# The first attention group opens on its short row tiles, with the bias fold moved to the last body

## The chip, the cores and the metric

The kernel runs on one core of a Trainium2 chip. The time is the device time of one launch, in microseconds (us), and the median of several runs is compared. The profile is of one further execution, and its times count from the start of that execution's span.

## The reference, cut to what matters

The input is x with 4 batches of 1024 rows of 128 features. A layer norm with modulation gives h. Then comes causal attention with 16 heads of size 8, whose scores have two parts:

```
scores = Q K^T / sqrt(8) + lambda * (tanh(Q) J) tanh(K)^T
scores = where(causal, -inf, scores)
probs  = softmax(scores);  out = probs V;  x = x + ga * (out Wo + bo)
```

A second norm gives each row to one of 8 experts, and row by row

```
ln = norm(xs) * gamma_e + beta_e
y  = xs + relu(ln W1_e^T + b1_e) W2_e^T + b2_e
```

is mixed back into x. Since beta_e only enters through W1_e, the product of W1_e with beta_e can be added to b1_e once and for all. That sum is the bias fold that the change moves.

## The kernel before, in words

**Groups and slots.** Each batch is one pass ("body"): batch 0 is the body "first", 1 and 2 are "middle", 3 is "last". A body has 4 groups of 4 heads. A group of attention is 12 units, and a unit is a pair of a query half `qc` (512 queries) and a block `kb` of 128 keys. Each unit has 4 slots, one a head, so that a group has 48 slots. Units 0 to 3 are the first query half, and so are slots 0 to 15. In a slot TensorE makes the transposed scores (L1258), adds the causal mask on diagonal blocks (L1262), and ScalarE takes the exponential (L1014). Two units later TensorE multiplies by the values (L1232).

**Maxima.** Before a group can start, the row maxima of its scores must be known, since they ride as three extra rows of the query stack into L1258. They are made by score products of another orientation (L1192), by chunks: a chunk is one or more heads of a row tile `t`, which has (t+1)*128 columns. Chunks with t from 4 to 7 are long (16 of them, one head each). VectorE reduces one with L1672. Chunks with t from 0 to 3 are short (6 of them, with 2 or 4 heads), reduced by L1679. After all 22 chunks of a group comes the step "T": TensorE turns the maxima (L1180), VectorE splits them into three bf16 terms (L1657 to L1663), and SyncE sends them into the stack (`send_maxima`, L426). TensorE waits for them with `m_in` in slot 0.

**The order around the change.** TensorE and VectorE each run one written-out order. `FIRST` is what comes before the first attention group: ten projections ("P": X0 to V1 of batch 0), the 22 chunks of group 0, two chunks of group 1, T of group 0, and four more chunks of group 1. Between them TensorE turns the expert weights (`turn_weights`, L1209), six after the projections and then one behind each chunk. ScalarE evacuates them, and SyncE stores them in two DMAs (L463). In a body, `schedule` places the next group's chunks behind slots, by a table of costs, and in group 0 also the ten projections of the next batch. ScalarE evacuates X, Q, K and J of those, and it makes the eight normalised row tiles of the next batch (L903) behind slots 1 and 3 of units 0 to 3.

**The fold.** GpSimd makes the folded bias in the prelude (`fold_beta`, L662 to L673) from W1, which is loaded for the turning, and from beta, which ScalarE's queue broadcasts into the tile `OT`. ScalarE waits for the fold (`b1_ok`) ahead of its first attention group, since it then writes `OT`, and GpSimd makes it ahead of its work on batches 0 and 1.

## Time and profile before

| | us |
|---|---|
| median of 3 runs (773.18 to 775.75) | 775.23 |
| the profiled execution | 773.26 |
| its span | 771.5 |
| TensorE busy | 676.7 (88%) |
| VectorE busy | 545.0 (71%) |
| ScalarE busy | 500.7 (65%) |
| GpSimd busy | 258.0 (33%) |

Read this as shares of the whole span. The stages differ: a prelude up to some 84 us, 16 attention groups up to some 640 us, and the expert part after that.

### The profile page before, as it was taken

What the parts mean: (1) busy time and instruction counts of PE and PEld (TensorE: products, weight loads), DVE (VectorE), ACT (ScalarE), POOL (GpSimd) and SP (SyncE); (2) the same over time, 40 slices, a digit from 0 to 9 for tenths busy, and PEclk for the clock granted to TensorE, in tenths of its full rate; (3) what the DMA queues carried; (4) which work ended last, traced back from release to release, by engine and by line L of the source; (5) the groups of instructions that cost most, each with busy time, mean ns of one, the idle gap of its engine ahead of it and who ended that gap; (6) DMA issues with size and microseconds to landing.
All of it is one profiled execution on the core that took longest, in us unless ns stands there. A gap on an engine that the chain in (4) does not pass through costs nothing.

```text
span 771.5 us, 15278 instructions
## 1 busy us (share of the span) xinstructions
PE 676.7 (88%) x5199; PEld 341.3 (44%) x5199; DVE 545.0 (71%) x1249; ACT 500.7 (65%) x1182; POOL 258.0 (33%) x342
## 2 busy tenths in 40 slices
PE   3657899999999998999999989999998989887693
PEld 2352344333333433433344434343443227886593
DVE  6959666887866786778667868788777603897352
ACT  1431577766767866766877586866767788655472
POOL 2009109200201943513138234210352202466443
PEclk9867699999999999999999999999999999999797
DMA  8996732456533251925606165636313445424610
GB/s 224 316 206 240 131 68 64 131 98 113 118 67 60 71 178 32 177 56 148 124 1 193 58 112 97 157 94 129 97 43 112 161 142 169 126 78 146 177 40 11
DMA packets 55572, 91.88 MB, mean 119 GB/s; under 512 B 10257, under 2 KB 26157, under 8 KB 55240
## 3 DMA queue, kind: packets, MB, share of 16 engines
q1 hardware_dynamic: 49308, 79.72, 41.6%
q0 software_dynamic: 3520, 8.42, 3.1%
q10 hardware_dynamic: 2668, 2.78, 1.3%
q8 instruction: 42, 0.69, 0.4%
q14 instruction: 34, 0.28, 0.1%
HBM read 51.04 MB, written 37.90 MB: 115 GB/s over the span
## 4 chain that ended last, share of the span: by engine, by line
PE 54%; DVE 20%; ACT 12%; issue 7%; DMA 4%; another core or an unknown queue 1%; ACTq 1%; DVEq 0%; POOL 0%; SPq 0%; POOLq 0%
PE PS L1232 15%; PE PS L1192 12%; PE PS L1258 11%; ACT arenaA L1014 7%; DVE PS L1672 6%; PE PS L1309 4%; PE PS L1320 3%; DVE block_max L1679 3%; ACT arenaB L932 2%; PE PS L1262 2%; DVE arenaA L1355 2%; DVE arenaB L1355 2%; PE PS L1197 1%; PE PS L1140 1%
## 5 line engine op out<-in xcount | busy, mean ns | idle before, releaser
L1014 ACT ACTIVATE arenaA<-PS 128x512 f32<-128x512 f32 (+3 forms) x768 | 332.4, 498 | 157.3 <-PE PS L1262 119.9
L1672 DVE CUSTOM_DVE_ANT_0 PS<-PS,mask 128x1024 f32<-128x1024 f32 (+3 forms) x256 | 261.4, 1035 | 90.4 <-PE PS L1192 85.4
L1258 PE MATMUL PS<-arenaA 99*128 99x512 bf16 (+3 forms) x768 | 221.5, 332 | 14.9 <-ACT arenaA L1014 11.6
L1192 PE MATMUL PS<-arenaA 96*128 96x512 bf16 (+3 forms) x768 | 198.8, 335 | 26.0 <-DVE maxima L1672 8.2
L1258 PEld LDWEIGHTS PS<-arenaA 99*128 99x128 bf16 x768 | 71.6, 97 | 202.5 <-ACT arenaA L1014 141.6
L1232 PE MATMUL PS<-arenaA,Vs 128*9 128x512 f32 (+3 forms) x1536 | 158.3, 488 | 0.0
L1679 DVE TENSOR_REDUCE block_max<-PS 128x8 f32<-128x1024 f32 (+1 forms) x96 | 100.4, 1045 | 28.8 <-PE PS L1197 26.1
L1192 PEld LDWEIGHTS PS<-arenaA 96*128 96x128 bf16 x768 | 66.7, 100 | 90.9 <-DVE maxima L1672 31.3
L1262 PE MATMUL PS<-after,identb 128*128 128x128 bf16 x512 | 104.5, 221 | 0.0
L1063 ACT ACTIVATE arenaA<-PS,b1p 128x128 f32<-128x128 f32 x184 | 52.6, 374 | 35.3 <-PE PS L1309 21.2
L831 POOL DMA_INDIRECT out_dram<-arenaA x46 | 46.1, 1002 | 82.7 <-DVE arenaA L1355 73.8
L1309 PE MATMUL PS<-arenaA 128*128 128x128 f32 x368 | 51.3, 284 | 11.8 <-DVE arenaA L1792 8.7
L1309 PEld LDWEIGHTS PS<-arenaA 128*128 128x128 f32 x368 | 45.4, 194 | 16.0 <-DVE arenaA L1792 12.3
L1320 PE MATMUL PS<-arenaA 128*128 x368 | 50.3, 282 | 1.9 <-issue 1.9
L1262 PEld LDWEIGHTS PS<-after,identb 128*128 128x128 bf16 x512 | 50.6, 99 | 2.3
L1197 PE MATMUL PS<-identb,after 128*128 128x128 bf16 x256 | 50.2, 224 | 0.0
L772 POOL DMA_INDIRECT by_expert<-arenaB,slot x24 | 23.5, 979 | 72.2 <-PE PS L1232 72.2
L1320 PEld LDWEIGHTS PS<-arenaA 128*128 128x128 f32 x368 | 46.1, 197 | 2.5 <-issue 2.4
L1232 PEld LDWEIGHTS PS<-arenaA,Vs 128*9 128x9 f32 x1536 | 24.6, 88 | 51.0 <-ACT arenaA L1014 26.2
L643 POOL TENSOR_TENSOR arenaB<-arenaB 128x1024 f32<-128x1024 f32 x12 | 25.6, 2133 | 55.6 <-ACT arenaB L873 55.6
L1355 DVE TENSOR_TENSOR arenaA<-PS,b_b 128x128 f32<-128x128 f32 x46 | 13.4, 290 | 33.6 <-PE PS L1320 21.7
L1672 DVE DVE_READ_ACCUMULATOR2_ANT maxima<- 128x1 f32 x256 | 35.7, 139 | 0.2
(219 smaller groups left out, 691.1 us busy)
## 6 DMA issues: line engine op xcount, KB each, us to landing
arenaA<-k_parts SPq DMA_DIRECT2D x96, 128.0 KB, 8.0
arenaA<-by_expert SPq DMA_DIRECT2D x46, 192.5 KB
o_raw<-OT SPq DMA_DIRECT2D x32, 256.0 KB, 2.1
k_parts<-arenaB SPq DMA_DIRECT2D x24, 256.0 KB, 3.8
arenaA<-q_parts SPq DMA_DIRECT2D x16, 384.0 KB, 5.2
q_parts<-arenaB SPq DMA_DIRECT2D x18, 256.0 KB, 3.8
arenaA<-in_L_ffn_W_dram SPq DMA_DIRECT2D x2, 2048.0 KB, 12.9
arenaA<-q_parts SPq DMA_DIRECT2D x16, 256.0 KB, 5.7
```

Of the source, the lines that this page charges most:

```text
L831: g.indirect_dma_start(out_rows, bass.IndirectOffsetOnAxis(ap=XSI[n % NX][:, 3 * D:3 * D + 1], axis=0), YS[:, n % U, :], None, bounds_chec ...
L1014: a.activation(PT[:, u % EB, h, off:HALF], PS[:, 4 + n % SB_, off:HALF], ACT.Exp).then_inc(exp_ok, 1)
L1063: last = a.activation(HR[:, n % 3, k * P:(k + 1) * P], PS[:, 3 + n % 2, k * P:(k + 1) * P], ACT.Relu, bias=b1p[:, bass.ds(expert[n] * FC + ...
L1192: last = mm(PS[:, place + c0 // HALF, at:at + c1 - c0], SQ(g, h)[0:KROWS, t * P:(t + 1) * P], SK(g, h)[0:KROWS, c0:c1], start=(at == 0), s ...
L1197: last = mm(diag, after[:, :], identb[:, :], start=False, stop=True, skip_group_check=True)
L1232: last = mm(PS[32 * h:32 * h + VW, 7, off:HALF], Vs[:, g, (kb * HG + h) * VW:(kb * HG + h + 1) * VW], PT[:, u % EB, h, off:HALF], start=(k ...
L1258: last = mm(bank[:, off:HALF], SK(g, h)[0:MROWS, kb * P:(kb + 1) * P], SQ(g, h)[0:MROWS, qc * HALF + off:(qc + 1) * HALF], start=True, sto ...
L1262: last = mm(bank[:, off:off + P], identb[:, :], after[:, :], start=False, stop=True, skip_group_check=True)
L1309: last = mm(PS[:, 3 + n % 2, k * P:(k + 1) * P], W1C[n % 3][:, k * P:(k + 1) * P], XT[:, n % 3, :], start=(k == 0), stop=True, skip_group_ ...
L1320: last = mm(PS[:, 6 + n % 2, 0:D], HR[:, n % 3, k * P:(k + 1) * P], W2T[:, bass.ds(expert[n] * FF + k * P, P)], start=(k == 0), stop=(k == ...
L1672: v.tensor_tensor_reduce(out=src, in0=src, in1=mask[:, S - n:S], scale=1.0, scalar=-3e38, op0=ALU.add, op1=ALU.max, accum_out=maxima[:, pl ...
L1679: v.tensor_reduce(block_max[:, place % 2, heads[0]:heads[-1] + 1, t, 0:t + 1], src.rearrange("p h (c q) -> p h c q", q=P), AX.X, ALU.max). ...
```

## The change

Four things are changed together.

1. `FIRST` now has the ten projections, the six short chunks of group 0, one long chunk, a new step "H", and four more long chunks. H turns and splits the maxima of the short tiles alone (from the new tile `first_max`), and `send_short_maxima` sends them in four DMAs, one a row tile, for queries 0 to 511. In the first group slot 0 waits for these (`m_short`).
2. The other 11 long chunks of group 0, two chunks of group 1, T of group 0 and four more chunks of group 1 are placed by hand behind slots 0 to 15 (`OPENING`), with five of the projections of batch 1 (X0, X1, Q0, Q1, K0). The wait for `m_in` stands ahead of slot 16. The remaining chunks of group 1 and five projections go behind slots 16 to 47. ScalarE's eight normalised tiles go behind slots 0 to 7.
3. The weights are turned two at a time behind the short chunks.
4. The bias fold is made in the last body. SyncE loads W1 again (four DMAs), beta and b2 there (`load_fold`), GpSimd folds after it has sent the rows of batch 2, and ScalarE waits for it ahead of the expert part. The broadcasts of beta and b2 at the start of the kernel are gone.

```diff
+        FOLD = 5120 + TB * ROWW
+        W1F = Bap[:, FOLD:FOLD + E * FF].rearrange("p (k d) -> p k d", d=D)
+        BETA = Bap[:, 4096:4096 + E * D]
+        FOLD_LOADS = 5
...
-        FIRST = [("P", 0, PREP.index(step)) for step in ("X0", "X1", "K0", "K1", "Q0", "Q1", "J0", "J1", "V0", "V1")] + [("m", 0, k) for k in range(NM)] + \
-                [("m", 1, 0), ("m", 1, 1), ("T", 0, 0)] + [("m", 1, k) for k in range(2, EARLY)]
-
+        SHORT = [k for k in range(NM) if CHUNKS[k][1] < 4]
+        LONG = [k for k in range(NM) if CHUNKS[k][1] >= 4]
+        AHEAD_LONG = 5
+        FIRST = [("P", 0, PREP.index(step)) for step in ("X0", "X1", "K0", "K1", "Q0", "Q1", "J0", "J1", "V0", "V1")] + [("m", 0, k) for k in SHORT] + \
+                [("m", 0, LONG[0]), ("H", 0, 0)] + [("m", 0, k) for k in LONG[1:AHEAD_LONG]]
+        HALF_SLOTS = 16
+        SOON = {"X0": 9, "X1": 10, "Q0": 12, "Q1": 13, "K0": 14}
+        LATER = dict(K1=1, V0=4, V1=7, J0=11, J1=13)
+        OPENING = [(n, "m", 0, k) for n, k in zip((0, 1, 2, 3, 5, 6, 7, 9, 11, 12, 14), LONG[AHEAD_LONG:])] + \
+                  [(14, "m", 1, 0), (14, "m", 1, 1), (15, "T", 0, 0)] + [(15, "m", 1, k) for k in range(2, EARLY)]
+        assert len(LONG) == 16
+        OPENING = sorted(OPENING + [(n, "P", 0, PREP.index(step)) for step, n in SOON.items()], key=lambda it: it[0])
...
+                fixed = opening if g == 0 else ()
...
+                if fixed:
+                    extra = [(at, "P", PREP.index(step)) for step, at in LATER.items()]
...
+                opens = HALF_SLOTS if fixed else 0
+                pace = early * (sum(SLOT_COST[opens:]) + sum(c[1] for c in cost)) / max(1, sum(c[0] for c in cost))
...
+            def send_short_maxima():
+
+                sp.wait_ge(max_used, FIRST.index(("H", 0, 0)) + 1 + MB_)
+                for t in range(4):
+                    sp.dma_start(stacks[KROWS:MROWS, 0, 0, :, t * P:(t + 1) * P], mrow[HG * TB + t:P:TB, :]).then_inc(m_short, 16)
...
-            send_maxima(0, T_FIRST)
+            send_short_maxima()
             sp.wait_ge(w_out, 32)
             for g in range(2, NG):
                 ones(g)
                 load_group(0, g)
+                if g == 2:
+                    send_maxima(0, dve_use("first", 0, next(it[0] for it in BODIES["first"][0][0] if it[2] == "T")))
...
+            def load_fold(group):
+
+                every = lambda v: v.rearrange("e d -> (e d)").rearrange("(a n) -> a n", a=1).to_broadcast([P, E * D])
+                for g in range(NG):
+                    sp.wait_ge(values_in[g], B * 16)
+                for k in range(W_PARTS):
+
+                    sp.wait_ge(pv_ok, group * NU + EB + 5 + k)
+                    some = slice(k * E // W_PARTS, (k + 1) * E // W_PARTS)
+                    sp.dma_start(W1F[:, k * E * FC // W_PARTS:(k + 1) * E * FC // W_PARTS, :].rearrange("p (e c) d -> p e (c d)", c=FC),
+                                 W1[some].rearrange("e (p c) d -> p e (c d)", c=FC)).then_inc(fold_in, 16)
+                sp.dma_start(BETA, every(beta)).then_inc(fold_in, 16)
+                sp.dma_start(b2_b[:, :], every(b2)).then_inc(b2_in, 16)
...
+                    if body == "last" and g == 1:
+                        load_fold(b * NG + g)
...
-                pool.wait_ge(beta_in, 16)
-                pool.wait_ge(b1_in, 16)
-                pool.wait_ge(w_ev, 8)
-                w1 = W1r.rearrange("p (e c) d -> p e c d", c=FC)
-                beta_b = OT[:, :, :].rearrange("p a q -> p (a q)").rearrange("p (e o d) -> p e o d", e=E, o=1).to_broadcast([P, E, FC, D])
+                pool.wait_ge(fold_in, FOLD_LOADS * 16)
+                w1 = W1F.rearrange("p (e c) d -> p e c d", c=FC)
...
-            pool.wait_ge(b1_ok, 1)
+            pool.wait_ge(b1_in, 16)
...
+            fold_beta()
...
-            act.dma_start(b2_b[:, :], row(b2.rearrange("e d -> (e d)")).to_broadcast([P, E * D])).then_inc(bias_in, 16)
             act.dma_start(b1c[:, :, :], b1.rearrange("e (p c) -> p e c", c=FC)).then_inc(b1_in, 16)
-            act.dma_start(OT[:, :, :].rearrange("p a q -> p (a q)"), row(beta.rearrange("e d -> (e d)")).to_broadcast([P, E * D])).then_inc(beta_in, 16)
...
+                        u, h = (t // 4, t % 4) if body == "first" else (t // 2, 1 + 2 * (t % 2))
+                        steps.setdefault((0, u), []).append((h, lambda b, t=t: norm_rows(b, t), 1))
...
-            act.wait_ge(b1_ok, 1)
...
+            act.wait_ge(b1_ok, 1)
...
+                if kind in "TH":
+                    pe.wait_ge(*((row_max, group + 1) if kind == "T" else (short_max, 1)))
                     for at in range(0, P, HG * TB):
-                        last = mm(PS[at:at + HG * TB, bank, 0:P], maxima[:, g, :], ident[:, :], start=True, stop=True)
+                        last = mm(PS[at:at + HG * TB, bank, 0:P], maxima[:, g, :] if kind == "T" else first_max[:, :], ident[:, :], start=True, stop=True)
...
-                for _ in range(6 if i == len(PREP) - 1 else 1 if i >= len(PREP) and turned_weights < 16 else 0):
+                for _ in range(6 if i == len(PREP) - 1 else min(2, 16 - turned_weights) if i >= len(PREP) else 0):
...
+                        if gi == 0 and u == 0:
+                            pe.wait_ge(m_short, 4 * 16)
+                        if u == (HALF_SLOTS // HG if gi == 0 else 0):
...
+                if k == SHORT[-1] and group == 0:
+                    dve.wait_ge(max_used, done)
+                    v.tensor_reduce(short_rows(first_max[:, :]), block_max[:, place % 2, :, :, :], AX.X, ALU.max).then_inc(short_max, 1)
```

TensorE, the end of the prelude, before: the last chunks of group 1, and then slot 0 (L1258 with its mask L1262). The waits are named in brackets.

```order
L1192 MATMUL PS<-arenaA 128x512 [waits max_used]
L1192 MATMUL PS<-arenaA 128x128
L1192 MATMUL PS<-arenaA 128x512 [waits max_used]
L1197 MATMUL PS<-identb,after 128x128
L1192 MATMUL PS<-arenaA 128x512
L1197 MATMUL PS<-identb,after 128x128
L1258 MATMUL PS<-arenaA 128x512 [waits m_in,mod_ok,exp_ok,w_ev,first_ones]
L1262 MATMUL PS<-after,identb 128x128
L1258 MATMUL PS<-arenaA 128x512 [waits exp_ok]
```

Slot 0 stood behind every chunk of `FIRST` and waited for `m_in`. TensorE at the same place now (L1218 is the turning of the maxima, L1230 a chunk, L1298 a slot, L1302 its mask):

```order
L1218 MATMUL PS<-ident,first_max 32x128 [waits short_max,max_used]
L1218 MATMUL PS<-ident,first_max 32x128 x3
L1230 MATMUL PS<-arenaA 128x512 [waits max_used]
L1230 MATMUL PS<-arenaA 128x128
L1230 MATMUL PS<-arenaA 128x512 [waits max_used]
L1230 MATMUL PS<-arenaA 128x128
L1230 MATMUL PS<-arenaA 128x512 [waits max_used]
L1230 MATMUL PS<-arenaA 128x128
L1230 MATMUL PS<-arenaA 128x512 [waits max_used]
L1230 MATMUL PS<-arenaA 128x256
L1298 MATMUL PS<-arenaA 128x512 [waits m_short,mod_ok,exp_ok,w_ev,first_ones]
L1302 MATMUL PS<-after,identb 128x128
```

Slot 0 now stands behind step H and four long chunks, and waits for `m_short`; 11 long chunks stand behind it, which stood ahead of it. TensorE around T of group 0 now, the projection K0 (L1167), slot 15 and T:

```order
L1167 MATMUL PS<-HT,wT 128x512 [waits max_used]
L1298 MATMUL PS<-arenaA 128x128 [waits exp_ok]
L1302 MATMUL PS<-after,identb 128x128
L1218 MATMUL PS<-ident,maxima 32x128 [waits row_max,max_used]
L1218 MATMUL PS<-ident,maxima 32x128 x3
```

And TensorE at slot 16, behind the last chunk of `OPENING` and the product with the values of unit 1 (L1270):

```order
L1230 MATMUL PS<-arenaA 128x512
L1235 MATMUL PS<-identb,after 128x128
L1270 MATMUL PS<-arenaA,Vs 9x384 [waits exp_ok]
L1270 MATMUL PS<-arenaA,Vs 9x384 x3
L1298 MATMUL PS<-arenaA 128x512 [waits exp_ok,m_in]
```

T stood four chunks ahead of the end of `FIRST`, without a slot before it. Now 16 slots stand before it, and the wait for `m_in` is at slot 16. SyncE's queue before, from the load of the values of group 1 on:

```order
L420 DMA Vs<-arenaB 128x288
L463 DMA w_turned<-arenaA 128x4096 [waits w_ev] x2
L426 DMA arenaA<-mrow 3x32x128 [waits max_used]
L398 DMA arenaA<-onesb 3x32x128 [waits w_out]
L410 DMA arenaA<-q_parts 48x4x1024
```

SyncE's queue now (L449 is the DMA of the short maxima, L486 the stores of the turned weights):

```order
L437 DMA Vs<-arenaB 128x288
L486 DMA w_turned<-arenaA 128x4096 [waits w_ev] x2
L449 DMA arenaA<-mrow 3x4x128 [waits max_used]
L449 DMA arenaA<-mrow 3x4x128 x3
L415 DMA arenaA<-onesb 3x32x128 [waits w_out]
L427 DMA arenaA<-q_parts 48x4x1024
```

The short maxima stand right behind the two stores of the turned weights, and T's maxima have moved behind the loads of group 2.

## Rows read from the trace of the kernel before

**Rows 1.** the page: busy time of each engine, share of the span, instructions

```profile
PE 676.7 (88%) x5199; PEld 341.3 (44%) x5199; DVE 545.0 (71%) x1249; ACT 500.7 (65%) x1182; POOL 258.0 (33%) x342
```

**Rows 2.** windows: stretch, its length, busy (instructions) of PE, PEld, DVE, ACT, POOL; PEclk, DMA share, GB/s

```profile
51.78:84.22 32.44, 25.83 (x134) 12.86 (x135) 28.34 (x52) 6.15 (x10) 21.83 (x14) 0.71 0.63 183
84.22:94.27 10.05, 9.73 (x63) 4.60 (x63) 5.65 (x9) 8.73 (x24) 0.00 (x0) 0.75 1.07 184
94.27:126.50 32.23, 30.50 (x206) 12.85 (x206) 20.24 (x42) 25.94 (x48) 12.92 (x7) 1.00 0.37 77
```

**Rows 3.** timeline where the first maxima are sent: start us, us, engine, line, op

```profile
79.10 0.29 DVE L1657 TENSOR_SCALAR mrow<-PS 128x128 bf16<-128x128 f32 x1
...
80.42 0.80 SPq L426 DMA_DIRECT2D arenaA<-mrow  x1
...
84.22 0.58 PE L1258 MATMUL PS<-arenaA 99*128 99x512 bf16 x1 [0.44 <-DMA arenaA<-mrow]
```

**Rows 4.** VectorE by form, 51.78 to 84.22: busy us, mean ns | idle before

```profile
L1672 DVE CUSTOM_DVE_ANT_0 PS<-PS,mask 128x640 f32<-128x640 f32 x7 | 5.8, 830 | 7.2 <-PE PS L1192 7.2
L1672 DVE CUSTOM_DVE_ANT_0 PS<-PS,mask 128x1024 f32<-128x1024 f32 x4 | 5.0, 1238 | 0.6 <-PE PS L1192 0.6
L1679 DVE TENSOR_REDUCE block_max<-PS 128x8 f32<-128x1024 f32 x4 | 4.9, 1223 | 0.6 <-PE PS L1197 0.5
L1672 DVE CUSTOM_DVE_ANT_0 PS<-PS,mask 128x896 f32<-128x896 f32 x4 | 4.5, 1122 | 0.3 <-PE PS L1192 0.3
L1672 DVE CUSTOM_DVE_ANT_0 PS<-PS,mask 128x768 f32<-128x768 f32 x4 | 3.9, 980 | 0.1
L1679 DVE TENSOR_REDUCE block_max<-PS 128x6 f32<-128x768 f32 x3 | 2.9, 958 | 0.2 <-PE PS L1197 0.2
```

**Rows 5.** line L463 on SyncE, the two stores of turned weights

```profile
L463 SPq DMA_DIRECT2D w_turned<-arenaA x2: 343/344/344, 55.8 to 63.1; - x2
...
DMA to landing us min/median/max: 9.2/10.4/11.6
```

**Rows 6.** windows, columns as in 2: the clock before and after its fall

```profile
64.00:68.70 4.70, 2.50 (x14) 0.92 (x14) 4.70 (x9) 0.00 (x0) 4.62 (x3) 1.00 1.02 436
68.70:89.20 20.50, 16.53 (x63) 5.59 (x64) 16.28 (x31) 3.71 (x9) 9.14 (x9) 0.50 0.39 86
```

**Rows 7.** timeline, 97 to 114: what single pieces of TensorE and ScalarE take

```profile
97.73 0.60 PE L1113 MATMUL PS<-ident,arenaB 128*128 128x128 f32 x4
...
106.46 1.04 PE L1232 MATMUL PS<-arenaA,Vs 128*9 128x512 f32 x8
...
107.66 0.60 PE L1192 MATMUL PS<-arenaA 96*128 96x512 bf16 x2
108.10 0.59 PE L1258 MATMUL PS<-arenaA 99*128 99x512 bf16 x2
108.53 1.02 PE L1129 MATMUL PS<-HT,wT 128*128 128x512 f32 x2
...
113.03 0.39 PE L1258 MATMUL PS<-arenaA 99*128 99x512 bf16 x1
...
113.31 0.38 PE L1258 MATMUL PS<-arenaA 99*128 99x512 bf16 x1
...
98.43 0.77 ACT L914 ACTIVATE HT<-PS,modT 128x512 f32<-128x512 f32 x1
```

**Rows 8.** timeline of GpSimd, SyncE and ScalarE: where the fold was, and will be

```profile
55.94 9.30 POOL L662 TENSOR_TENSOR arenaA<-arenaA,OT 128x1024 f32<-128x1024 f32 x4 [50.18 <-ACT arenaA L985]
...
75.79 0.26 POOL L673 TENSOR_TENSOR b1p<-arenaA,b1c 128x32 f32<-128x32 f32 x1
...
578.50 0.78 SPq L426 DMA_DIRECT2D arenaA<-mrow  x1
...
612.79 0.96 POOL L772 DMA_INDIRECT by_expert<-arenaB,slot  x1 [1.10 <-PE PS L1232]
...
640.84 1.14 ACT L1050 ACTIVATE arenaA<-arenaA 128x512 f32 x2
```

More of the change, by code:

```diff
@@ L256, in build, with schedule @@
         BEST_IN = dict(middle=2, last=1)
-        def schedule(prep, post, last):
+        def schedule(prep, post, last, opening=()):
             groups, n = [], 0
@@ L271, in schedule @@
                 early = 0.82 if last and g == NG - 2 else 1.0
-                pace = early * (sum(SLOT_COST) + sum(c[1] for c in cost)) / max(1, sum(c[0] for c in cost))
+                opens = HALF_SLOTS if fixed else 0
+                pace = early * (sum(SLOT_COST[opens:]) + sum(c[1] for c in cost)) / max(1, sum(c[0] for c in cost))
                 slots, clock, m = [], 0, 0
-                for i in range(NU * HG):
+                for i in range(opens, NU * HG):
                     clock += SLOT_COST[i]
@@ L280, in schedule @@
                 items = []
-                for m, (kind, ahead, k) in enumerate(seq):
-                    items.append((n, slots[m], kind, (g + ahead) % NG, ahead, k))
+                for at, kind, ahead, k in list(fixed) + [(slots[m], *it) for m, it in enumerate(seq)]:
+                    items.append((n, at, kind, (g + ahead) % NG, ahead, k))
                     n += kind != "D"
@@ L285, in schedule @@
             return groups, n
-        BODIES = dict(first=schedule(True, STATS_AT, False), middle=schedule(True, POST_AT, False), last=schedule(False, POST_LAST, True))
+        BODIES = dict(first=schedule(True, STATS_AT, False, OPENING), middle=schedule(True, POST_AT, False), last=schedule(False, POST_LAST, True))
         N0 = len(FIRST)
@@ L514, in attention @@
                         load_reciprocals(b - 1)
+                    if body == "last" and g == 1:
+                        load_fold(b * NG + g)
                     if body != "last" or g + 1 < NG:
-                        t_use = next(it[0] for it in BODIES[body][0][g] if it[2] == "T")
+                        t_use = next(it[0] for it in BODIES[body][0][g] if it[2] == "T" and it[4] == 1)
                         send_maxima((g + 1) % NG, dve_use(body, b, t_use))
@@ L669, in fold_beta @@
                         part = slice(k * E * FC // chunks, (k + 1) * E * FC // chunks)
-                        g.tensor_tensor(W1r[:, part, 0:half], W1r[:, part, 0:half], W1r[:, part, half:2 * half], ALU.add).then_inc(b1_step, 1)
+                        g.tensor_tensor(W1F[:, part, 0:half], W1F[:, part, 0:half], W1F[:, part, half:2 * half], ALU.add).then_inc(b1_step, 1)
                     half //= 2
                 pool.wait_ge(b1_step, done + chunks)
-                g.tensor_tensor(b1p[:, :], W1r[:, :, 0], b1c[:, :, :].rearrange("p e c -> p (e c)"), ALU.add).then_inc(b1_ok, 1)
-            fold_beta()
+                g.tensor_tensor(b1p[:, :], W1F[:, :, 0], b1c[:, :, :].rearrange("p e c -> p (e c)"), ALU.add).then_inc(b1_ok, 1)
             def residual(b):
@@ L1183, in maximum @@
                 heads, t = CHUNKS[k]
-                if k == 0:
+                if k == 0 or loads == 0 and g == 0 and k == SHORT[0]:
                     pe.wait_ge(stack_in[g], (loads + 1) * 9 * 16)
@@ L1386, in _ @@
             v.memset(block_max[:, :, :, :, :], -3e38)
+            v.memset(first_max[:, :], 0.0)
+            short_rows = lambda columns: columns.rearrange("p (h t) -> p h t", h=HG)[:, :, 0:4]
             def batch_stats(b):
@@ L1793, in _ @@
             last_table = tile_table(1)
+            dve.wait_ge(b2_in, 16)
             for n in range(TURNS):
```

28 lines of the change are left out of this document (14 added, 14 removed).

## The prediction

> **What bounds the kernel now.** I read the page first. TensorE is busy for 88% of the span and VectorE for 71% [rows 1], so on average a change has to free TensorE. But the change works in one stage, so I cut the trace by stage [rows 2]. From 51.78 us (the first chunk of group 0) to 84.22 (slot 0) VectorE is busy 28.34 of 32.44 us, with ScalarE nearly idle at 6.15: VectorE's maxima bound this stage. From 84.22 to 94.27 (slots 0 to 15) VectorE has only 5.65 of 10.05, while TensorE has 9.73 and ScalarE 8.73. From 94.27 to 126.50 (slots 16 to 47) TensorE has 30.50 of 32.23. So the idea is sound: slots of the second stage go beside the maxima of the first. Most that this could give is the second stage's own 10.05 us. The timeline shows what links the stages: VectorE starts T's four operations at 79.10, the DMA is issued at 80.42, and slot 0 starts at 84.22 [rows 3], 3.80 us behind the issue.
>
> I measure the change by when slot 16 starts (before: 94.27), and by how long slots 16 to 47 take from there (before: 32.23). Later groups keep their order, and TensorE stays near full, so that the sum of both differences lasts to the end.
>
> **When slot 0 can start.** VectorE has for H six short reductions of at most 1.22 us [rows 4], one long one of 0.83, the small one and four operations of H of some 1.5 us (T took 1.32, rows 3's starts). From 51.78 that gives 61 to 62 us, if TensorE keeps up. It doesn't quite, since it turns two weight tiles behind each short chunk; I estimate 66. But that doesn't decide. The short maxima stand in SyncE's queue behind two stores of 2 MB each. They were issued at 55.8 and 63.1, and landed after 11.6 and 9.2 us [rows 5], so the second landed at 72.3. A DMA that is issued behind them on the same queue can hardly land sooner. The stores start no later than before, and the loads ahead of them are the same. I take **slot 0 at 72.4**, 11.8 us sooner. If the small DMAs could pass the stores, it would be 66 + 3.8 = 69.8; I keep that end.
>
> **What VectorE loses.** Only four more long chunks are written ahead of slot 0. With 66 for H, three of 0.83 and one of 0.98 us [rows 4] keep VectorE busy until about 69.5. The next chunk stands behind slot 0 in TensorE's order, so that VectorE's next work is ready at about 72.4 + 0.5 (slot) + 0.7 (chunk) = 73.6: some 4 us idle on the engine that bounds the stage. From there it has 11 long chunks (3 x 0.98 + 4 x 1.12 + 4 x 1.24 = 12.4, of which about 0.9 overlaps between neighbours, which I take from their starts: 11.5), the small reduction 0.2, two chunks of group 1 (1.5), and T 1.3: 14.5, so T's DMA is issued at 88.1 at best and **slot 16 starts at 88.1 + 3.8 = 91.9 at best**.
>
> **What TensorE has to do in the same stretch.** Prices are at the full clock, from starts [rows 7]: a 512-column slot with mask 0.28 (113.03 to 113.31), the shorter ones by columns 0.23, 0.17 and 0.12, so 16 slots 3.2. A chunk of 1024 columns 0.44 (107.66 to 108.10), by columns 0.39 and 0.33: 11 long ones 4.3. X0 and X1 0.5 each (record 0.60), Q0, Q1 and K0 1.0 each (record 1.02): 4.0. The values of unit 0: 1.0. Two chunks of group 1 and T's turning: 1.1. Sum 13.6. The clock was down, at 0.50, for 68.70 to 89.20, behind a stretch in which TensorE was busy 2.50 of 4.70 us [rows 6]. It will be as sparse before slot 0 now, and I take slots from 72.4 at half clock for 5 us, as from 84.22 to 89.20 before: 2.5 more. 72.4 + 16.1 = 88.5 for T's turning.
>
> **What ScalarE has to do.** Slots 0 to 15 with the eight normalised tiles took 8.73 us of it [rows 2]. Now all eight tiles stand behind slots 0 to 7, and Q0 waits for both halves of X, 0.77 each [rows 7]. Without the last four exponentials (about 0.9) that is 9.4, from 73.1: Q0 starts at 82.5 at best. Behind it come on TensorE Q0, Q1, K0 (3.0), three slots (0.4), the last long chunk, two of group 1 and T (1.5): T's turning at 87.4 at best.
>
> So three engines each need until 87.4 to 88.5 for T, in one written order with two chunk buffers and three score banks between them. They can't all be at their best. Laying the pieces out one after another with their waits, I get T's turning at about 91, its DMA at 92.3, and **slot 16 at 96.0**. That is 1.7 us later than before, between the ends of 91.9 and some 98.
>
> **Slots 16 to 47.** TensorE's 30.50 us [rows 2] lose X0, X1, Q0, Q1, K0 (4.0) and gain five chunks of group 1 that used to stand behind slots 2 to 13 (0.28 to 0.54 each, 2.1): 28.6. VectorE's 20.24 gain those five reductions (0.83, 0.96, 0.98, 1.12, 1.22 = 5.1 [rows 4]): 25.3. With 28.6 and 25.3 in one order the wait is more than the 1.7 of before; I take 2.2: **30.8, or 1.4 us less**. Ends: 29.5 and 33.
>
> **The other parts.** The broadcasts of beta and b2 leave the first 20 us; there VectorE's chain bounds the kernel and waits for none of them, and the first chunk waits for the stack at 51.78. I cost it at 0, at most 0.3 gained. The fold took from 55.94 to 76.05 on GpSimd, 20.1 us [rows 8], beside other work. Now it can start when the rows of batch 2 have landed, about 3 us behind 612.79, and ends at about 636. ScalarE needs it for the expert part at 640.84 [rows 8]: 4.8 us to spare, and each us beyond that would be paid in full. On SyncE the loads for it (3 MB) wait for units of group 13 and are issued well ahead of T's maxima at 578.50 [rows 8]. I cost that at 0. ScalarE's and GpSimd's early wait for the fold goes; slot 0 never waited for it.
>
> **Sum.** +1.7 - 1.4 = +0.3 us, against the profiled execution's 773.26: 773.6. The median of the runs shown lies 2.0 above that execution, so 775.5.
>
> **The rivals.** (A) *Slots and maxima interleave well.* Slot 16 starts at 93 and the rest takes 29.8: -1.3 - 2.4 = -3.7, or 771.5. For it: the sum of any one engine allows 91.9, and ScalarE has less to do behind slot 16. Against it: the 4 us in which VectorE waits for slot 0. It needs T's DMA issued by 90, and decides from slot 16 at 94 on.
>
> (B) *The clock falls a second time, and the kernel is slower.* Between T's turning and slot 16 TensorE has four chunks and the values of unit 1, about 2.4 us of work in 5. Ahead of the fall at 68.70 it had 2.50 in 4.70 [rows 6]. Before the change, slots 16 to 47 ran at 1.00 throughout [rows 2]. At half clock for 5 to 7 us TensorE loses 2.5 to 3.5: +0.3 + 2.9 = +3.2, or 778.4. It decides when the clock is down for more than 4 us behind slot 16. On this the Trainium skill has a rule (TensorE: Matmul & The Clock Gate, "HAM oscillation — how this bites in real kernels"): a kernel that waits for a DMA between bursts of matmuls runs the start of each burst at half clock. The trace agrees for slot 0, where 84.22 to 89.20 ran at 0.50 behind a wait for the maxima. The rule speaks against this change, which has two such waits (slots 0 and 16) where there was one; by it (B) would be the likeliest.
>
> (C) *The fold is late* by 1 to 3 us, because GpSimd is slower beside the table steps of VectorE or the rows land late: 777 to 778. The 4.8 us to spare speak against it.
>
> **How the numbers follow.** The forecast 0.40 (its own range 774 to 777.5), (A) 0.28, (B) 0.27, (C) 0.05. About 0.3%, 2.3 us, is what a measurement of this kernel can tell from no change. (A) lies mostly beyond it on the fast side, (B) and (C) mostly on the slow side, with a little of each within: faster 0.27, same 0.43, slower 0.30. The range goes from (A) with slot 16 at 92.5 to (B) with 7 us of low clock: 770.8 to 779.2.
>
> **What the profile after would show.** Slot 0 (the first L1298) at 72.4, behind a DMA from `mrow`; 69.8 would say that the small DMAs passed the stores. VectorE idle for about 4 us ahead of 73.6. T's DMA at 92.3 and slot 16 at 96.0. TensorE at 1.00 behind it (forecast) or at 0.50 (B). Slot 47 near 126, and the shift there the same at 640. The fold's last operation on GpSimd near 636, with ScalarE's L1050 pieces not waiting. The prediction is wrong if slot 16 lies outside 94 to 98, if the rest takes less than 29.5 or more than 32.5, or if later groups give back or lose what the first one shifts.

## The result: 793 us, 18 us slower

| | before | after |
|---|---|---|
| median, us | 775.2 | 793.0 |
| profiled execution, us | 773.26 | 793.46 |
| its span, us | 771.5 | 791.7 |

The ratio is 1.0234, with a 95% interval of 1.0216 to 1.0253. The prediction was 775.5 us. Two of the six executions of the changed kernel and one of the six of the kernel before were far slower than the rest (832.7, 967.3 and 872.4 us) and don't count in the ratio; the medians of the others are 792.4 and 775.2. The work is nearly the same, as the page's busy line of the changed kernel shows beside [rows 1] (TensorE 2.4 us more): the loss is in waits.

```profile
PE 679.1 (86%) x5207; PEld 345.2 (44%) x5207; DVE 546.3 (69%) x1255; ACT 501.3 (63%) x1182; POOL 258.2 (33%) x342
```

The windows of the changed kernel, with the columns of [rows 2]. They are cut at slot 0, at slot 16, and at the issue of the maxima of group 1:

```profile
51.78:72.98 21.20, 13.09 (x90) 9.49 (x90) 12.07 (x21) 5.71 (x10) 0.00 (x0) 0.74 0.96 271
72.98:98.02 25.04, 21.06 (x115) 8.89 (x115) 19.14 (x36) 12.46 (x29) 2.35 (x1) 0.84 0.49 84
98.02:135.11 37.09, 28.95 (x184) 12.18 (x180) 22.17 (x45) 21.81 (x38) 22.43 (x12) 0.88 0.30 47
```

Before slot 0 VectorE is busy for 12.07 us of 21.20. Slot 16 starts at 98.02, 3.75 behind the 94.27 of [rows 2]. The last stretch, up to the maxima of group 1, takes 37.09 us.

Where the shift arises is read from SyncE's timeline: each DMA from `mrow` is the maxima of one group. First those of groups 1 and 15 of the kernel before (that of group 14 is in [rows 8], at 578.50; that of group 13 went at 541.34):

```profile
122.11 0.74 SPq L426 DMA_DIRECT2D arenaA<-mrow  x1
...
608.65 0.73 SPq L426 DMA_DIRECT2D arenaA<-mrow  x1
```

And in the changed kernel (group 13 at 553.75), with the loads for the fold (L536 to L539):

```profile
135.11 0.74 SPq L443 DMA_DIRECT2D arenaA<-mrow  x1
...
578.18 10.81 SPq L536 DMA_DIRECT2D arenaB<-in_L_ffn_W_dram  x4
...
590.24 0.43 SPq L539 DMA_DIRECT2D b_b<-in_L_ffn_b_dram  x1
590.91 0.77 SPq L443 DMA_DIRECT2D arenaA<-mrow  x1
...
626.56 0.73 SPq L443 DMA_DIRECT2D arenaA<-mrow  x1
```

The shift is 13.0 us at group 1, 12.4 at groups 13 and 14, and 17.9 at group 15. So it comes in two places: the opening, and between the maxima of groups 14 and 15. The groups between neither give back nor lose much.

**First place.** The timeline of the changed kernel, with SyncE (SPq), TensorE (PE) and VectorE (DVE) together. L449 sends the short maxima, L443 those of T, L437 loads the values of a group (here group 3, the last of `load_group`), L1298 is a slot, and L1395 (the line of a helper) here adds the bias to V and writes `VA`:

```profile
65.36 3.09 SPq L449 DMA_DIRECT2D arenaA<-mrow  x4
...
72.98 0.58 PE L1298 MATMUL PS<-arenaA 99*128 99x512 bf16 x1 [5.00 <-DMA arenaA<-mrow]
...
74.61 1.10 DVE L1717 CUSTOM_DVE_ANT_0 PS<-PS,mask 128x896 f32<-128x896 f32 x1 [5.42 <-PE PS L1230]
...
94.11 0.73 SPq L443 DMA_DIRECT2D arenaA<-mrow  x1
...
98.02 1.46 PE L1298 MATMUL PS<-arenaA 99*128 99x512 bf16 x3
...
99.90 0.54 SPq L437 DMA_DIRECT2D Vs<-arenaB  x1
...
109.16 0.88 DVE L1395 TENSOR_TENSOR arenaB<-PS,bv_b 128x128 f32<-128x128 f32 x4 [5.75 <-DMA Vs<-arenaB]
...
110.10 0.93 PE L1230 MATMUL PS<-arenaA 96*128 96x512 bf16 x2 [5.38 <-DVE arenaB L1395]
```

Slot 0 came at 72.98, near the predicted 72.4, and T's DMA went out at 94.11. What stands in no step of the prediction is the wait at 109.16. VectorE's part of V0 (values of batch 1) overwrites the buffer from which SyncE's loads read the values of batch 0, so that it waits for the loads of all four groups (`values_in`). The load for group 3 was issued at 92.78 before the change, ahead of which stood T's DMA at 80.42 [rows 3]. Now T's DMA is 14 us later, the load stands behind it and behind group 3's queries and keys at 99.90, and V0 is written earlier in the order. VectorE idles for 5.75 us and TensorE for 5.38. The windows show the clock: ahead of slot 16, at slot 16, in the wait at V0, behind it, and in the last row behind the wait of the second place:

```profile
88.50:96.70 8.20, 5.34 (x43) 2.21 (x45) 6.65 (x15) 1.79 (x5) 0.00 (x0) 1.00 0.03 7
96.70:100.10 3.40, 3.40 (x13) 0.98 (x14) 1.24 (x2) 1.44 (x3) 0.00 (x0) 0.50 1.00 187
104.30:110.10 5.80, 0.42 (x3) 0.03 (x2) 0.94 (x5) 1.54 (x2) 3.65 (x2) 0.73 0.60 78
110.10:113.50 3.40, 3.40 (x14) 2.41 (x15) 2.33 (x6) 0.60 (x1) 2.49 (x2) 0.50 0.00 0
598.50:602.00 3.50, 3.50 (x18) 1.27 (x18) 0.89 (x2) 2.76 (x7) 0.00 (x0) 0.52 0.00 0
```

The clock (the column ahead of the last two) fell to half twice around this place. It was at 0.50 from 96.70 to 100.10, across slot 16, behind a stretch in which TensorE was busy for 5.34 of 8.20 us and waited for VectorE and ScalarE in pieces of 0.7 us at most, for no DMA. It fell again during the wait at V0 (0.73 on average from 104.30 to 110.10) and was still at 0.50 behind it.

**Second place.** Group 14 starts on the kernel's fifteenth maxima. Its first slot, in TensorE's timeline of the kernel before and of the changed kernel, and the DMA's own piece in the changed kernel's chain of waits (start, us):

```profile
581.98 0.39 PE L1258 MATMUL PS<-arenaA 99*128 99x512 bf16 x1
```

```profile
598.49 0.61 PE L1298 MATMUL PS<-arenaA 99*128 99x512 bf16 x1 [4.03 <-DMA arenaA<-mrow]
```

```profile
590.91 7.53 DMA arenaA<-mrow
```

The four loads of W1, each waiting for a unit, occupy SyncE's queue from 578.18 to 589, and the two broadcasts until 590.7. The maxima are issued right behind them and take 7.53 us to land, twice as long as T's DMA in [rows 3] (3.80 to slot 0). VectorE had the maxima ready at 590.9, so the queue didn't hold back the issue here, only the landing. TensorE waits.

### The profile page after: what moved, and what is told of

It is laid out like the page before. It is cut to its first block, busy times and chain, and to the rows that moved or that the text cites. A ratio compares the mean times of both kernels' runs of the same rounds, so it can differ in the third digit from the quotient of the medians.

```text
span 791.7 us, 15315 instructions
## 1 busy us (share of the span) xinstructions
PE 679.1 (86%) x5207; PEld 345.2 (44%) x5207; DVE 546.3 (69%) x1255; ACT 501.3 (63%) x1182; POOL 258.2 (33%) x342
## 4 chain that ended last, share of the span: by engine, by line
PE 53%; DVE 19%; ACT 10%; DMA 7%; issue 6%; SPq 1%; another core or an unknown queue 1%; DVEq 0%; ACTq 0%; POOL 0%; POOLq 0%
PE PS L1270 14%; PE PS L1298 12%; PE PS L1230 12%; ACT arenaA L1050 6%; DVE PS L1717 6%; PE PS L1349 3%; PE PS L1360 3%; DVE block_max L1724 3%; PE PS L1302 2%; DVE arenaA L1395 2%; ACT arenaB L969 2%; DVE arenaB L1395 2%; DMA arenaA<-mrow 2%; PE PS L1235 1%; DMA arenaB<-r_den 1%
## 5 line engine op out<-in xcount | busy, mean ns | idle before, releaser
L1298 PE MATMUL PS<-arenaA 99*128 99x512 bf16 (+3 forms) x768 | 223.7, 335 | 23.3 <-ACT arenaA L1050 11.2
L1230 PE MATMUL PS<-arenaA 96*128 96x512 bf16 (+3 forms) x768 | 197.1, 333 | 32.1 <-DVE block_max L1724 7.3
L1298 PEld LDWEIGHTS PS<-arenaA 99*128 99x128 bf16 x768 | 71.7, 98 | 212.9 <-ACT arenaA L1050 139.1
L1270 PE MATMUL PS<-arenaA,Vs 128*9 128x512 f32 (+3 forms) x1536 | 159.2, 490 | 0.0
L1230 PEld LDWEIGHTS PS<-arenaA 96*128 96x128 bf16 x768 | 66.4, 100 | 92.6 <-DVE maxima L1717 23.5
L1302 PE MATMUL PS<-after,identb 128*128 128x128 bf16 x512 | 105.0, 222 | 0.0
L1349 PE MATMUL PS<-arenaA 128*128 128x128 f32 x368 | 52.8, 289 | 10.4 <-DVE arenaA L1840 7.7
L1349 PEld LDWEIGHTS PS<-arenaA 128*128 128x128 f32 x368 | 47.2, 201 | 14.0 <-DVE arenaA L1840 10.8
L1302 PEld LDWEIGHTS PS<-after,identb 128*128 128x128 bf16 x512 | 50.8, 99 | 4.4 <-issue 1.6
L1360 PEld LDWEIGHTS PS<-arenaA 128*128 128x128 f32 x368 | 47.2, 201 | 2.3 <-issue 2.2
L1270 PEld LDWEIGHTS PS<-arenaA,Vs 128*9 128x9 f32 x1536 | 24.6, 88 | 51.5 <-ACT arenaA L1050 25.8
L718 POOL TENSOR_TENSOR X<-X,ga_bo 128x1024 f32<-128x1024 f32 x4 | 9.4, 2346 | 107.3 <-ACT arenaB L940 66.9
L1395 DVE TENSOR_TENSOR arenaA<-PS,b_b 128x128 f32<-128x128 f32 x46 | 13.3, 289 | 35.8 <-PE PS L1360 24.1
```

Source lines behind the costliest of these rows:

```text
L1230: last = mm(PS[:, place + c0 // HALF, at:at + c1 - c0], SQ(g, h)[0:KROWS, t * P:(t + 1) * P], SK(g, h)[0:KROWS, c0:c1], start=(at == 0), s ...
L1270: last = mm(PS[32 * h:32 * h + VW, 7, off:HALF], Vs[:, g, (kb * HG + h) * VW:(kb * HG + h + 1) * VW], PT[:, u % EB, h, off:HALF], start=(k ...
L1298: last = mm(bank[:, off:HALF], SK(g, h)[0:MROWS, kb * P:(kb + 1) * P], SQ(g, h)[0:MROWS, qc * HALF + off:(qc + 1) * HALF], start=True, sto ...
L1302: last = mm(bank[:, off:off + P], identb[:, :], after[:, :], start=False, stop=True, skip_group_check=True)
L1349: last = mm(PS[:, 3 + n % 2, k * P:(k + 1) * P], W1C[n % 3][:, k * P:(k + 1) * P], XT[:, n % 3, :], start=(k == 0), stop=True, skip_group_ ...
L1360: last = mm(PS[:, 6 + n % 2, 0:D], HR[:, n % 3, k * P:(k + 1) * P], W2T[:, bass.ds(expert[n] * FF + k * P, P)], start=(k == 0), stop=(k == ...
```

## The experiments

Two theories stood against each other. By the **queue theory** the two waits cause most of the loss, each since one DMA stands behind another in SyncE's queue. By the **opening theory** the new order of the first group is slow by itself, and the waits are where it shows. All times below are medians; the ratio is to the kernel before, run beside them on the same chip (773.2 to 774.4 us). A difference between two of these ratios is known to about 0.3%, some 2 us.

| run | built on | us | ratio (95%) |
|---|---|---|---|
| loads_first | changed kernel | 785.3 | 1.0144 (1.0117 to 1.0171) |
| values_late | changed kernel | 784.9 | 1.0144 (1.0124 to 1.0164) |
| fold_behind | changed kernel | 786.6 | 1.0169 (1.0149 to 1.0189) |
| both | changed kernel | 781.0 | 1.0094 (1.0074 to 1.0113) |
| fold_only | kernel before | 780.2 | 1.0080 (1.0061 to 1.0098) |
| fold_free | kernel before | 774.0 | 1.0002 (0.9991 to 1.0013) |
| more_ahead | both | 781.5 | 1.0106 (1.0085 to 1.0126) |
| stores_behind | both | 780.6 | 1.0082 (1.0057 to 1.0107) |
| ahead_stores | both | 777.3 | 1.0049 (1.0030 to 1.0068) |
| filled | ahead_stores | 778.7 | 1.0051 (1.0033 to 1.0070) |
| filled_first | filled | 779.0 | 1.0069 (1.0052 to 1.0086) |
| mixed | ahead_stores | 782.8 | 1.0100 (1.0078 to 1.0123) |
| mixed_early | mixed | 778.5 | 1.0059 (1.0045 to 1.0073) |
| ahead_early | ahead_stores | 789.1 | 1.0197 (1.0181 to 1.0213) |

### The wait at V0: loads_first, values_late, and ahead_early

```
-                if g == 2:
+                if g == NG - 1:
                     send_maxima(0, dve_use(...))          # loads_first
```

> The loads of group 3 stand ahead of T's maxima in SyncE's queue instead of behind them; nothing else differs from the changed kernel (793.0 us). Queue theory: VectorE's part of V0 waited 5.75 us for the values of group 3, whose load was issued at 99.90, behind T's DMA. Now it is issued near 84, V0 doesn't wait, TensorE's 5.4 us of idle time ahead of 110.10 goes, and so does the half clock of 110.10 to 113.5 (1.7 us): about 7 us less, 786. Opening theory (the rival): the first group is slow because its order packs badly after slot 16 and V0 only happened to be where it showed; then the wait moves elsewhere and the time stays above 790.

```
-        LATER = dict(K1=1, V0=4, V1=7, J0=11, J1=13)
+        LATER = dict(K1=1, V0=9, V1=12, J0=14, J1=16)     # values_late
```

> SyncE's queue is as in the changed kernel, but V0 and V1 of the next batch (and J0, J1 behind them) are written about as late among the slots as before the change. Queue theory: V0 is ready later than the load of group 3 lands (about 109), so TensorE and VectorE have chunks and slots to do meanwhile; 5 to 7 us less, 786 to 788. Opening theory: above 790.

Both took 7.0 us off the loss (from 2.34% of some 774 us to 1.44%). Timeline of loads_first, SyncE and VectorE:

```profile
83.30 0.54 SPq L437 DMA_DIRECT2D Vs<-arenaB  x1
...
103.65 0.88 DVE L1395 TENSOR_TENSOR arenaB<-PS,bv_b 128x128 f32<-128x128 f32 x4 [0.80 <-PE PS L1159]
...
128.34 0.73 SPq L443 DMA_DIRECT2D arenaA<-mrow  x1
```

The load goes out at 83.30, V0 is worked on at 103.65 behind 0.80 us of waiting for TensorE, and the maxima of group 1 go at 128.34 instead of 135.11. In values_late VectorE still waits for the values, but 2.62 instead of 5.75 us, and the maxima of group 1 go at 130.94.

A later run is the counter-test. It moves T's DMAs ahead of the loads of both groups and leaves V0 where it is:

```
             for k in range(2): ...store of w_turned
+            send_long_maxima(...)
             sp.wait_ge(w_out, 32)
             ones(2)
             load_group(0, 2)
-            send_long_maxima(...)
```

> Built on the run with eight long chunks ahead and the stores behind (777.3 us): only the place of T's DMAs is changed, from behind the loads of group 2 to ahead of them. They were ready at 86.5 there and issued at 86.53, so the queue didn't hold them; if they wait for nothing but VectorE, slot 16 moves by at most the data ahead of them in flight (about 2 us), and V0 then waits for group 3's values, whose loads go out later: 777 to 780. If the transfers ahead of them held slot 16: 775.

```profile
100.97 0.54 SPq L437 DMA_DIRECT2D Vs<-arenaB  x1
...
115.77 0.88 DVE L1403 TENSOR_TENSOR arenaB<-PS,bv_b 128x128 f32<-128x128 f32 x4 [12.29 <-DMA Vs<-arenaB]
...
138.32 0.75 SPq L443 DMA_DIRECT2D arenaA<-mrow  x1
```

It came out far worse than expected: the load is issued at 100.97, VectorE waits 12.29 us for it, and the run takes 12 us more than ahead_stores, though its slot 16 came no later (94.28 against 94.97). So the same wait, made longer, costs more. The queue theory holds for the first place. I had named this wait in the expectation and sized it far too low.

### The fold: fold_behind, both, fold_only, fold_free

```
-                    if body == "last" and g == 1:
-                        load_fold(b * NG + g)
                     if body != "last" or g + 1 < NG:
                         ...
                         send_maxima((g + 1) % NG, dve_use(body, b, t_use))
+                    if body == "last" and g == 1:
+                        load_fold(b * NG + g)
```

> The six loads for the fold are issued behind the maxima of group 14 instead of ahead of them, 3 MB as before. Queue theory: the maxima DMA lands 3.8 us behind its issue instead of 7.6, TensorE doesn't idle the 4.0 us ahead of 598.49 and keeps its clock (another 1.3): 5.5 us less, 787.5; the fold still ends ahead of the expert part, since it starts only behind the rows of batch 2. Contention theory (the rival): 3 MB of loads cost what they cost wherever they stand, by slowing the stores, the weights' return and the row scatters: less than 2 us less, above 791.

> Both moves together: group 3's loads ahead of T's maxima, the fold's loads behind the maxima of group 14. Queue theory: the two add up, 12.5 us less than the changed kernel, 780.5; what is left over the kernel before (5 us) is the opening itself, whose slot 16 came 3.75 us late. If the opening theory holds for the first group, 787 or more.

The measured gains are 5.0 us for fold_behind and 10.8 for both moves. Both agree with the queue theory within 2 us. Next the fold was moved alone, the opening being that of the kernel before: fold_only with the loads where the change has them, fold_free with the edit above.

> The kernel before, with only the fold and its loads moved into the last body, as the change does it (loads ahead of the maxima of group 14). The opening is that of the kernel before. Queue theory: the maxima DMA of group 14 lands late again and costs 5.5 us, 779 where the kernel before takes 773.2; the first 580 us keep their times. Rival: GpSimd's 20 us of early work slowed the beginning and its going gives something back, or the loads only hurt together with the new opening: within 2 us of before.

> The kernel before with only the fold moved into the last body, its loads behind the maxima of group 14. Queue theory: the fold costs nothing there and its going from the beginning gives nothing, within 1 us of the kernel before. Rival: GpSimd's and the DMA engines' extra work around 600 us costs something by itself: 1 to 3 us slower.

SyncE's maxima of groups 1, 14 and 15 in fold_only, to be read beside the rows of before:

```profile
121.99 0.74 SPq L430 DMA_DIRECT2D arenaA<-mrow  x1
...
578.87 0.78 SPq L430 DMA_DIRECT2D arenaA<-mrow  x1
...
614.10 0.73 SPq L430 DMA_DIRECT2D arenaA<-mrow  x1
```

Group 1 is where it was, group 14 is 0.4 us later, group 15 5.45. The fold alone costs 6.2 us with its loads ahead of the maxima, and nothing with the same 3 MB behind them. The rival (the extra loads and GpSimd's work cost something wherever they stand) falls. Whether the maxima landed late because of their place in SyncE's own queue, or because 3 MB kept the DMA engines busy just then, is not told apart: no run put the loads on another queue. The removal of the fold from the beginning gave nothing either.

### What is left of the opening

The run with both moves is still 7.3 us behind the kernel before. Its maxima of groups 1, 14 and 15, with the fold's loads now behind those of 14:

```profile
130.17 0.73 SPq L443 DMA_DIRECT2D arenaA<-mrow  x1
...
585.61 0.78 SPq L443 DMA_DIRECT2D arenaA<-mrow  x1
586.57 1.92 SPq L536 DMA_DIRECT2D arenaB<-in_L_ffn_W_dram  x4
...
615.77 0.73 SPq L443 DMA_DIRECT2D arenaA<-mrow  x1
```

The shift is 8.1 us at group 1, and 7.1 at groups 14 and 15, so all of it arises in the opening. Windows over the same times, first of the kernel before, then of both:

```profile
51.78:73.00 21.22, 17.78 (x100) 10.43 (x100) 18.32 (x31) 6.15 (x10) 16.83 (x8) 0.82 0.91 268
73.00:95.00 22.00, 18.52 (x101) 7.42 (x101) 16.00 (x30) 9.09 (x25) 5.61 (x8) 0.63 0.59 101
95.00:122.00 27.00, 25.41 (x161) 10.55 (x159) 17.43 (x37) 21.99 (x38) 7.97 (x5) 1.00 0.32 59
```

```profile
51.78:73.00 21.22, 13.01 (x90) 9.39 (x90) 12.07 (x21) 5.72 (x10) 0.00 (x0) 0.74 1.04 276
73.00:95.00 22.00, 17.57 (x96) 7.89 (x96) 15.11 (x30) 12.43 (x29) 2.35 (x1) 0.85 0.93 149
95.00:122.00 27.00, 22.62 (x125) 8.29 (x126) 19.34 (x37) 15.44 (x25) 14.05 (x7) 0.94 0.09 21
```

From 51.78 to 73 VectorE is busy 12.07 us instead of 18.32, and TensorE 13.01 instead of 17.78. Both are short of work there. The short chunks stand by themselves, where each gives VectorE little to do for what it costs TensorE (products, masks, two weight tiles), and from 69.5 on both wait for the short maxima.

The third rows differ in the clock too, 1.00 and 0.94. The run with both moves has the same fall at slot 16 as the changed kernel, and the kernel before has none there:

```profile
96.90:100.30 3.40, 3.24 (x14) 0.80 (x15) 2.13 (x4) 0.01 (x1) 0.00 (x0) 0.50 0.05 13
```

By my estimate these 3.4 us at half clock are worth 1.7 us, if TensorE bounds the stage there. It isn't the whole of the 7: filled, below, stays at 1.00 from 80 us on, and is no faster for it.

Several ways to fill the lack of work were tried, on top of both.

```
-        AHEAD_LONG = 5
+        AHEAD_LONG = 9            # more_ahead; seven chunks and T behind slots 0 to 9
```

This run also cuts T's DMA in four, one a long row tile, as the short one is, and so do all later runs with the new opening but stores_behind.

> Built on the run with both moves (781.0 us). Eight long chunks instead of four stand behind H, ahead of slot 0, so that VectorE has work while the short maxima are on their way (it idled 6.35 us ahead of 75.96); the other seven and T stand behind slots 0 to 9, and T's DMA, cut in four like the short one, writes only the long row tiles. If VectorE's idle time ahead of slot 0 is what the opening costs: T's DMA is issued near 86 instead of 95.2, slot 16 starts near 92 instead of 99, and most of that lasts: about 776. Rival: the cost is in how chunks, slots and preparing steps share the banks and the ScalarE turns; then slots 0 to 15 themselves end late, slot 16 moves by 2 us or less, and the time stays above 779.

```
+            send_short_maxima()
             for k in range(2): ...store of w_turned
-            send_short_maxima()
             sp.wait_ge(w_out, 32)      # stores_behind; then group 2's loads, T's DMA, group 3's loads
```

This run also has V0 and V1 late, as in values_late.

> Built on the run with both moves (781.0 us), with V0 and V1 late as well. The two stores of 2 MB stand behind the short maxima in SyncE's queue instead of ahead of them; T's DMA stands between the loads of groups 2 and 3. If the stores hold back the short maxima (issued at 65.4, landed at 73): slot 0 starts near 69.5, 3.5 us sooner, and T's DMA at most as much sooner: 778. Rival: slot 0 comes sooner but T's DMA doesn't, since it waits for VectorE's maxima, or the stores land so late that the loads behind them and T's DMA are late: 781 or more.

The third run of this set, ahead_stores, has both edits.

> The last two together. If VectorE bounds the opening, it is never without work now from 52 to T, and T's DMA would be ready near 83 to 84; but it waits in SyncE's queue for the stores (landed near 83) and for the loads of group 2 (5 us more): slot 16 near 94, 776. If the two gains simply added: 773. Rival as before: above 779.

Alone neither gave anything that can be told apart from both (stores_behind had one execution at 786.96 among its four, the profiled one). Together they gave 3.5 us back. In more_ahead T's DMAs were issued from 87.01 on, 8 us sooner, but slot 16 started at 97.42. Of these 10.4 us 3.0 are the issue of the four pieces, where the single DMA of the changed kernel took 0.73 to issue and slot 16 followed 3.9 behind (94.11 to 98.02). The rest I put down to the loads of group 3, whose last was issued 2 us ahead: another case of the same queue, though no run tells the two apart. Next, chunks where VectorE still idled behind T:

```
-        HALF_SLOTS = 16
+        HALF_SLOTS, MORE = 16, 5   # five more chunks of group 1 behind slots 9 to 15, out of those behind slots 16 to 47
```

V0, V1, J0 and J1 stand a little sooner here (7, 11, 12, 14 instead of 9, 12, 14, 16). filled_first is the same with the stores ahead of the short maxima again.

> Built on the last of the runs before (eight long chunks ahead, stores behind; 777.3 us), with five more chunks of group 1 written between slots 9 and 15, where VectorE ran out of work (4.2 us ahead of 98.30, 1.5 ahead of 91.17). Idle theory: what the opening costs is VectorE's idle time up to the maxima DMA of group 1, 20.9 us there against 18.5 before; filling 4 us of it puts that DMA at 121.5 to 122 (before 122.11) and the time at 773 to 774, the same as the kernel before. Rival: the chunks only delay slots 9 to 15 on TensorE, slot 16 moves back by as much as is gained behind it, 777.

> As the run above, but with the two stores of 2 MB ahead of the short maxima, as in the changed kernel. The group 2 loads then go out at 73 to 79 instead of 79 to 85 and have landed when T's DMAs are issued near 87, but slot 0 is at 73 instead of 71.4. If the transfers ahead of T's DMAs decide slot 16, it comes sooner than in the run above: 772. If slot 0 decides, 775.

Nothing: the maxima of group 1 went at 125.50 against 125.67, and slot 16 at 99.84 against 94.97. The rival held there: the chunks only moved other work. The last idea was the beginning itself.

```
-[("m", 0, k) for k in SHORT] + [("m", 0, LONG[0]), ("H", 0, 0)] + ...
+[("m", 0, k) for pair in zip(SHORT, LONG) for k in pair] + [("H", 0, 0)] + ...   # mixed
```

H stands behind these twelve chunks, and one weight tile is turned behind each instead of two.

> Built on the run with eight long chunks ahead and the stores behind (777.3 us). The six short chunks of group 0 alternate with six long ones again, as before the change, and one weight tile is turned behind each; H stands behind the twelfth chunk, five more long ones behind it, the last five and T behind slots 0 to 7. Theory: written by themselves the short chunks starve VectorE (busy 12.07 of 21.20 us ahead of slot 0 in the changed kernel), since they cost TensorE more than VectorE. Mixed, H is ready near 67 and VectorE has two or three chunks more behind it when slot 0 starts near 72.5: T's DMAs at 84 instead of 86.5, slot 16 near 93, 775. Rival: H later by 2 us puts slot 0 back by 2 us and eats it: 777 or more.

```profile
51.78:73.00 21.22, 17.11 (x104) 10.46 (x104) 17.96 (x32) 6.40 (x11) 0.00 (x0) 0.82 0.60 108
73.00:95.00 22.00, 16.62 (x100) 7.70 (x100) 13.00 (x26) 12.52 (x29) 2.35 (x1) 0.85 0.90 249
95.00:122.00 27.00, 23.02 (x127) 8.94 (x128) 17.51 (x34) 18.07 (x30) 17.04 (x9) 0.94 0.35 66
```

VectorE's 18 us of the first stretch are back (17.96), and yet the run is no faster: 782.8, by its median slower than ahead_stores. Its six executions spread from 777.9 to 783.3, and the profile is of one of the two fast ones (779.28), so that what slowed the other four isn't seen. T's maxima were ready at 84.2, but their DMAs went out at 88.23 behind the loads of group 2, and slot 16 waited for them until 96.5. What VectorE gained ahead of slot 0 it lost behind it: 13.00 us busy from 73 to 95, against 16.00.

The last run, mixed_early, sends T's DMAs ahead of the loads of groups 2 and 3, and moves V0 and V1 later (14 and 16) and J0 and J1 sooner (9 and 11).

> Built on the mixed run (its profile: T's maxima ready at 84.2, their DMAs issued at 88.2, slot 16 at 96.5). T's four DMAs stand ahead of the loads of groups 2 and 3 in SyncE's queue, and V0, V1 are written later still, since those loads go out about 3 us later. If SyncE's queue is what holds slot 16 once VectorE is kept busy, slot 16 starts near 91, 5 us sooner, and the time is 773 to 775, that of the kernel before. Rival: TensorE and ScalarE bound slots 0 to 15 with the preparing steps (they ended at 92 in the mixed run), slot 16 moves by 2 us or less there and the order behind it isn't faster: 777 or more.

TensorE's timeline of mixed_early at slot 16 (L1306) and at J0, J1 (L1161), and its clock from there:

```profile
93.37 0.82 PE L1306 MATMUL PS<-arenaA 99*128 99x512 bf16 x3
...
105.45 2.07 PE L1161 MATMUL PS<-arenaB,JL 128*128 128x512 f32 x2 [2.25 <-ACT arenaB L963]
```

```profile
104.90:111.70 6.80, 6.21 (x20) 3.56 (x21) 2.42 (x3) 2.64 (x5) 6.64 (x4) 0.50 0.83 162
```

Slot 16 came at 93.37 without a wait for a DMA: there TensorE's own row of slots, preparing steps and values is the bound. That is 0.9 us sooner than before the change, but the kernel before had by then eleven chunks of group 1 behind it, this one six. And J0, J1, moved up for V0, waited 2.25 us for ScalarE, and the clock fell to 0.50 for 6.8 us there. Slots 25 and 26 had started 4.3 us sooner than in mixed (101.12 against 105.44); slot 47 came only 1.0 sooner (127.10 against 128.13). The 3.3 us between are what 6.8 us at half clock cost by my estimate (3.4). So most of what T's DMAs had gained went at this place, and the expected 773 to 775 wasn't reached. The same order with J0 and J1 later wasn't run.

## Why the prediction was wrong

- **Slot 0 at 72.4**: 72.98, behind the DMA from `mrow`, at half clock. Right, and for the reason given (the stores ahead in the queue): from the first issue to slot 0 it took 7.6 us here (65.36 to 72.98), and 4.4 in stores_behind (67.00 to 71.42).
- **VectorE idle for 4 us ahead of 73.6**: 5.42 ahead of 74.61. Right in kind.
- **T's DMA at 92.3, slot 16 at 96.0**: 94.11 and 98.02, at the far end of the range that I gave (91.9 to 98). The term was +1.7 and measured +3.75. The half clock behind slot 0, which I took at 5 us, lasted until 79.6, 6.7 us.
- **"Slots 16 to 47 ... 30.8, or 1.4 us less"**: this is the first step that failed. I summed TensorE's and VectorE's work and took 2.2 us for waits. From slot 16 to the maxima of group 1 it took 37.09 us, where the kernel before took 27.84 (122.11 - 94.27): 9.25 more. Up to the first slot of group 1, where my stretch ends within a us, it is 41.15 against 32.92 us (139.17 and 127.19 less slot 16): the term of -1.4 measured +8.2. Some 7 us of it is V0's wait with the clock's fall behind it, as loads_first shows. I had dated T's DMA 12 us later without asking what stands behind it on SyncE, and who waits for that.
- **"issued well ahead of T's maxima at 578.50"** of the loads for the fold: the second step that failed. They wait for units whose products fall at 578 to 590, and the last of them went out 0.7 us ahead of the maxima. It cost 5.5 us in the profile, 5.0 to 6.2 by the runs.
- **The fold**: it ended at 654.64, 636.7 without the shift of 17.9, and ScalarE's expert part waited for TensorE, not for it. Rival (C) falls, in the timeline of GpSimd and ScalarE:

```profile
634.41 9.30 POOL L701 TENSOR_TENSOR arenaB<-arenaB 128x1024 f32<-128x1024 f32 x4 [2.75 <-DMA by_expert<-arenaB,slot]
...
654.38 0.26 POOL L712 TENSOR_TENSOR b1p<-arenaB,b1c 128x32 f32<-128x32 f32 x1
...
660.39 1.14 ACT L1101 ACTIVATE arenaA<-PS,b1p 128x128 f32<-128x128 f32 x4 [0.50 <-PE PS L1349]
```

- **Broadcasts gone: 0.** Right (fold_free).
- **Rival (B), a second fall of the clock at slot 16, for 5 to 7 us:** there in kind, and shorter. The clock was at 0.50 from 96.70 to 100.10, 3.4 us, of which 2.1 lie behind slot 16, under the 4 us that I had set as its sign; at half clock that is 1.7 us of TensorE's work, not 2.5 to 3.5. The forecast's "TensorE at 1.00 behind it" was wrong. The clock also fell behind two waits that no rival had: it was at 0.50 from 110.10 to 113.50 and at 0.52 from 598.5 to 602.0. The rule of the Trainium skill cited with (B) (TensorE: Matmul & The Clock Gate, "HAM oscillation — how this bites in real kernels") has a wait for a DMA and then a burst at half clock, and the trace agrees for these two waits. The fall at slot 16 came without a wait for a DMA. And the half clock at 84.22 in the kernel before, which I took for an instance of the rule, had begun at 68.70 [rows 6]; TensorE waited only 0.44 us for the maxima there [rows 3].
- **The sum**: +0.3 was predicted. In the profile +13.0 (group 1), -0.6 until group 14, +5.5, and 2.3 more in the expert part. The last, the expert part's, isn't explained. From the maxima of group 15 to the end the profiled executions took 162.9 (before), 162.5 (fold_free), 163.6 (both), 164.9 (fold_only) and 165.1 us (after), and the medians differ by 17.8 us, not 20.2, since the profiled execution before lay 2.0 us below its median and the one after 0.5 above.

Together: of 18 us, 7 are V0's wait, 5 to 6 the fold's loads, and some 7 the opening, less 1 or 2 by which they overlap. Of the opening's 7 it is shown that both TensorE and VectorE lack work ahead of slot 0, and that filling it there moves the lack to slots 0 to 47. The half clock at slot 16 is worth up to 1.7 of it. That the preparing steps bound slots 0 to 15 is read from one trace (mixed_early) and was not tested by a run that takes them out. No version with the new opening beat the kernel before; the best was ahead_stores, 0.5% behind it. That the opening could win with another order is open.
